# Loading the first seven blocks of grouped rows in attention's last slot instead of at the start of the expert phase

## What is computed

```
x = layernorm(x + attention(x))
x = layernorm(x + cross_attention(x, ctx))
scores = (x @ router_w.T + router_b) / temp          # 8 numbers for each token
gates  = sinkhorn(scores, 3 iterations)              # over groups of tokens and experts
top 2 gates of each token, divided by their sum
y[token] = sum over its 2 experts e: gate * ((relu(x @ wg[e]) * (x @ wp[e])) @ wo[e])
x = layernorm(x + (x + y))
```

## Time and profile before

| what | value |
|---|---|
| median of 3 runs | 991.87 us (991.46 to 995.86) |
| the profiled execution, its own time | 997.48 us |
| its span, first to last instruction | 995.7 us |
| outside the span (997.48 - 995.7) | 1.78 us |
| attention, up to the barrier | 0 to about 788 us |
| expert phase | about 788 us to the end |
| TensorE busy | 875.5 us, 88% of the span |
| mean granted TensorE clock | 0.947 of full speed |

### The profile page before, as it was taken

How to read it: one execution, slowest core, us unless ns; L and a number is a source line. 1 busy time by engine, 2 the same in 40 slices (tenths; PEclk the granted TensorE clock), 3 DMA queues, 4 the chain that set the end, 5 groups by cost and what they waited for, 6 DMA issues and landing times. The chain is left out here.

```text
span 995.7 us, 23083 instructions
## 1 busy us (share of the span) xinstructions
PE 875.5 (88%) x6694; PEld 680.1 (68%) x6694; DVE 733.4 (74%) x2148; ACT 686.6 (69%) x2423; POOL 566.7 (57%) x862
## 2 busy tenths in 40 slices
PE   4999999999999999999999987899997499989830
PEld 3777777777777777777777766677775366767620
DVE  3578888888888888888887888888886267645655
ACT  3687888878888888888887885687884154535410
POOL 5665555555555555555555554788884034777371
PEclk8999999999999999999999999899997599989975
DMA  4990000000000000000000000010000321142223
GB/s 126 253 102 11 10 8 8 8 10 8 8 13 8 8 8 8 8 11 8 9 13 6 10 9 7 20 34 31 24 21 20 84 72 36 51 136 97 67 91 116
DMA packets 63299, 39.17 MB, mean 39 GB/s; under 512 B 15904, under 2 KB 60192, under 8 KB 63232
## 3 DMA queue, kind: packets, MB, share of 16 engines
q1 hardware_dynamic: 58688, 28.89, 13.1%
q0 software_dynamic: 4544, 9.45, 2.8%
HBM read 21.51 MB, written 16.81 MB: 38 GB/s over the span
## 5 line engine op out<-in xcount | busy, mean ns | idle before, releaser
L458 ACT ACTIVATE prob<-ps,negmax 128x128 f32<-128x128 f32 x512 | 181.3, 413 | 9.5 <-DVE negmax L577 9.5
L378 POOL TENSOR_TENSOR prob<-prob,recip 128x512 f32<-128x512 f32 x128 | 136.9, 1078 | 42.4 <-DVE recip L582 42.3
L466 ACT ACTIVATE xprob<-ps,xmax 128x128 f32<-128x128 f32 x512 | 144.8, 421 | 20.0 <-DVE xmax L577 20.0
L387 POOL TENSOR_TENSOR qk_sin<-qk,sin_sb 128x128 f32<-128x128 f32 x256 | 115.5, 471 | 59.4 <-ACT qk L445 59.0
L458 ACT ACTIVATION_READ_ACCUMULATOR prob<-ps,negmax 128x1 f32 x512 | 130.0, 254 | 0.0
L577 DVE TENSOR_REDUCE xmax<-ps 128x4 f32<-128x512 f32 x128 | 87.3, 689 | 33.2 <-PE ps L866 32.9
L1475 POOL DMA_INDIRECT answered<-ysb,goes_to x78 | 76.3, 978 | 57.6 <-DVE ysb L1557 40.8
L445 ACT ACTIVATE qk<-ps 128x512 f32<-128x512 f32 x128 | 74.1, 605 | 49.3 <-PE ps L783 49.2
L393 POOL TENSOR_TENSOR qk<-qk_cos,qk_sin 128x256 f32<-128x256 f32 x128 | 94.5, 739 | 20.2 <-DVE qk_cos L586 20.2
L402 POOL TENSOR_TENSOR ve<-mv,eps 128x1 f32<-128x1 f32 x64 | 12.1, 189 | 159.2 <-DVE mv L600 158.8
L781 PE MATMUL ps<-w_lo,xT_hi 128*128 128x512 f32 x192 | 91.4, 476 | 7.4 <-DVE xT_lo L611 7.4
(11 more groups left out here) (204 smaller groups left out, 2253.4 us busy)
## 6 DMA issues: line engine op xcount, KB each, us to landing
xg<-placed SPq DMA_DIRECT2D x8, 528.0 KB, 7.5
yq<-answered SPq DMA_DIRECT2D x8, 512.0 KB, 3.9
placed<-blank_x SPq DMA_DIRECT2D x1, 3008.0 KB, 26.5
xf<-in_x SPq DMA_DIRECT2D x32, 64.0 KB, 1.9
xres<-in_x SPq DMA_DIRECT2D x32, 64.0 KB
cx<-in_ctx SPq DMA_DIRECT2D x32, 64.0 KB, 1.8
out_y<-yo SPq DMA_DIRECT2D x8, 256.0 KB, 2.4
placed<-blank_x SPq DMA_DIRECT2D x1, 1984.0 KB, 23.2
```

The costliest lines, as they stand in the source:

```text
L378: nc.gpsimd.tensor_tensor(prob[:, n], prob[:, n], recip[:, n, :, None].broadcast_to([128, 4, S]), ALU.mult).then_inc(normed, 1)
L387: last = nc.gpsimd.tensor_tensor(sines[:, :, side, :], part[:, :, 1 - side, :], table, ALU.mult)
L458: last = nc.scalar.activation(prob[:, n, j, :], bank(name)[:, j * S:(j + 1) * S], ACT.Exp, bias=negmax[:, n, j:j + 1], accum_out=sums[:, n ...
L466: last = nc.scalar.activation(xprob[:, n, g, :], bank(name)[:, g * S:(g + 1) * S], ACT.Exp, bias=xmax[:, n, g:g + 1])
```

## The change

Seven blocks of group 0 (`AHEAD = 7`) get a buffer of their own, `xg_first`, of 128 x 7 x 132 numbers. It is allocated with the buffers that live through the whole program, and so is the semaphore `first_loaded`. SP waits for `scattered[0]` and issues the load into it in slot `B + 2`, before the barrier; this wait leaves the expert phase. The chunks of group 0 are now blocks 0 to 6, 7 to 14, 15 to 22, 23 to 30, 31 to 38 and 39 to 46, where they were 0 to 7, 8 to 15 and so on; there are still six, of which five are issued in the expert phase. `xg0` is smaller by seven blocks. A helper `rows` picks the buffer for a block. All buffers allocated behind `xg_first` start 3.7 KB further on in each partition, up to those behind `xg0`.

```
+AHEAD = 7
...
+        xg_first = keep("xg_first", [128, AHEAD, ROW])
+        first_loaded = sem("first_loaded")
...
+                if isinstance(s, int) and s == B + 2:
+                    sp.wait_ge(scattered[0], 16 * 2 * plan.size[0])
+                    sp.dma_start(xg_first[:], placed[0][0:AHEAD * 128, :].rearrange("(n p) d -> p n d", p=128)).then_inc(first_loaded, 16)
...
-        xg = [sb(f"xg{g}", [128, plan.blocks[g], ROW]) for g in range(G)]
+        xg = [sb(f"xg{g}", [128, plan.blocks[g] - (AHEAD if g == 0 else 0), ROW]) for g in range(G)]
+
+        def rows(g, c0, c1):
+
+            if g == 0:
+                return xg_first[:, c0:c1, :] if c1 <= AHEAD else xg[0][:, c0 - AHEAD:c1 - AHEAD, :]
+            return xg[g][:, c0:c1, :]
+
...
-        chunks = [(g, c, min(c + CHUNK, plan.blocks[g])) for g in range(G) for c in range(0, plan.blocks[g], CHUNK)]
+        chunks = [(0, 0, AHEAD)]
+        chunks += [(g, c, min(c + CHUNK, plan.blocks[g])) for g in range(G) for c in range(0 if g else AHEAD, plan.blocks[g], CHUNK)]
...
-        xg_loaded = [sem(f"xg_loaded{n}") for n in range(len(chunks))]
+        xg_loaded = [first_loaded] + [sem(f"xg_loaded{n}") for n in range(1, len(chunks))]
...
             for n, (g, c0, c1) in enumerate(chunks):
-                if c0 == 0:
+                if n == 0:
+                    continue
+                if g and c0 == 0:
                     sp.wait_ge(scattered[g], 16 * 2 * plan.size[g])
-                sp.dma_start(xg[g][:, c0:c1, :], placed[g][c0 * 128:c1 * 128, :].rearrange("(n p) d -> p n d", p=128))\
+                sp.dma_start(rows(g, c0, c1), placed[g][c0 * 128:c1 * 128, :].rearrange("(n p) d -> p n d", p=128))\
                     .then_inc(xg_loaded[n], 16)
...
             def x_transpose(i):
                 g = plan.group_of[i]
+                j = i - plan.block0[g]
                 pe.wait_ge(xg_loaded[chunk_of[i]], 16)
                 wait(pe, lo_done, i)
-                nc.tensor.transpose(ps[:, XT, 0:128], xg[g][:, i - plan.block0[g], 0:D], ident[:]).then_inc(xt_filled, 1)
+                nc.tensor.transpose(ps[:, XT, 0:128], rows(g, j, j + 1)[:, 0, 0:D], ident[:]).then_inc(xt_filled, 1)
```

More of the change, by code:

```diff
@@ L107, in decoder_layer @@
                         [(temp_sb[:], temp), (eidx_sb[:], eidx)], tri, ones, fw_hi, fw_lo, fwo_sb,
-                        f_loaded, fo_loaded, f_hi, f_lo, fwg, fwp, fwo, plan, routing, placed, cleared, scattered)
-        ffn_phase(nc, sem, ps, routing, plan, x2_all, fw_hi, fw_lo, fwo_sb, ident, mhalf, eps, f_lo, fo_loaded, placed, answered,
+                        f_loaded, fo_loaded, xg_first, first_loaded, f_hi, f_lo, fwg, fwp, fwo, plan, routing, placed, cleared, scattered)
+        ffn_phase(nc, sem, ps, routing, plan, x2_all, fw_hi, fw_lo, fwo_sb, ident, mhalf, eps, f_lo, fo_loaded, xg_first, first_loaded, placed, answered,
                   cleared, scattered, out)
@@ L114, in attention_phase @@
                     xcos, xsin, ident_d, causal_d, gsel_d, wqkv, wo, xwq, xwkv, xwo, rw, rb, also_loaded, tri, ones,
-                    fw_hi, fw_lo, fwo_sb, f_loaded, fo_loaded, f_hi, f_lo, fwg, fwp, fwo, plan, routing, placed, cleared, scattered):
+                    fw_hi, fw_lo, fwo_sb, f_loaded, fo_loaded, xg_first, first_loaded, f_hi, f_lo, fwg, fwp, fwo, plan, routing, placed, cleared, scattered):
     with ExitStack() as phase:
@@ L1358, with ffn_phase @@
 DISPATCH_SLOT = _s + 1
-def ffn_phase(nc, sem, ps, routing, plan, x2_all, fw_hi, fw_lo, fwo_sb, ident, mhalf, eps, f_lo, fo_loaded, placed, answered,
+def ffn_phase(nc, sem, ps, routing, plan, x2_all, fw_hi, fw_lo, fwo_sb, ident, mhalf, eps, f_lo, fo_loaded, xg_first, first_loaded, placed, answered,
               cleared, scattered, out):
```

8 lines of the change are left out of this document (4 added, 4 removed).

## The result

The changed kernel takes 991.80 us in the median of 14 runs (986.98 to 992.27). The kernel before, run beside it, takes 994.53 us (14 runs, the three known beforehand among them, 991.24 to 997.72). The ratio is 0.9965, with a 95% interval of 0.9948 to 0.9981. That is 3.5 us less, the distance of the means (the medians are 2.7 us apart), and within the 0.5% that the prediction calls no change. The predicted gain, 0.40%, is inside the interval. The predicted time, 987.9 us with a range of 985.6 to 990.6, is not: 991.80 lies 1.2 us above its upper end.

What follows compares the result with a forecast made beforehand. The prediction took PE's wait for xg's load between attention and block 0, with everything behind it hanging on block 0, to bound the kernel. Terms 4.0 + 0 + 0 + 0 + 0 = 4.0 us gave 987.9 us, range 985.6 to 990.6.

Steps and rivals of the forecast that it cites:

- What bounds the kernel: Between attention and block 0, PE waits 6.49 us: barrier and register load keep 2.5, the load of xg alone 4.0.
- The load leaves the hole: Issued on SP before the barrier at about 773.1 us, it lands by 778 to 782.5; PE's wait shrinks by 4.0 us.
- The terms taken at nothing: Other loads, SP's wait for the scatters, meta one block earlier, the clock, and buffers 3.7 KB further on: 0 each.
- The five other loads: Issued behind the barrier from 788.43 us; blocks 7 to 14 land with 5 to 9 us of slack, cost 0.
- The clock: At the expert phase's start, PE's lower clock level lasts 4.5 us as before, cost 0; bounds 1.7 gained, 1.5 lost.
- the clock stays low longer: Rival, start of expert phase: clock rises at 798.0 us as before, gain shrinks to 2.5 us, 989.4 us; 14%.
- Code behind the barrier: Rival: ACT or DVE must fetch instructions for block 0 behind the barrier, gain 1.6 to 3.2 us, 989.5 us; 8%.
- The gain doesn't reach the end: Rival: group 1's scatters or the sends behind them go by something else than block 0, gain 0, 991.9 us; 7%.
- the last sentence of the sum: Whole kernel: the same 4.0 us subtracted from the median of the runs, 991.87 - 4.0 = 987.9 us, 0.40% less.

Runs made afterwards that it cites:

- the after trace with the late clock: The changed kernel, unchanged, timed and profiled again against the kernel before: 990.14 us (12 runs), ratio 0.9946; in its trace the clock rose 9.3 us after b0.
- The filler: The kernel before plus 18 matmuls that nothing reads, in slots 33 and 34 where PE waits: 989.85 us (11 runs), ratio 0.9941.

## Why the prediction was right, and where it was wrong

**What bounds the kernel: right.** The hole, the barrier in it and the register load behind it were read as they are. After: the barrier opened 1.39 us after attention's last matmul, as before, and the transpose came 786.68 - 785.55 = 1.13 us later, where the prediction said 1.1.

**The load leaves the hole: right.** 3.97 us against 4.0. The last scatter of group 0 started at 769.57 and the load was issued at 771.88, 2.31 us later, where the prediction had 2.29. It landed in 3.6 us where the rows had offered 5.0 to 9.4: those loads had others beside them, this one had none. The slack made the difference harmless.

**The terms taken at nothing: right.** Undoing the load's place alone gave 1.0005, which bounds buffers, addresses and `meta` together. The five other loads land in 5.3 to 8.5 us, and PE had no wait at block 7:

```profile
L1461 SPq DMA_DIRECT2D xg<-placed x5: 373/1007/2947, 785.6 to 790.7; - x5
...
DMA to landing us min/median/max: 5.3/7.2/8.5
```

The experiment with one block ahead shows what stood behind this zero: with too few blocks the next load is late and the gain is gone.

**The clock: the stretch too short, its price too high.** The stretch at the lower level behind b0 was taken at the 4.5 us of before. It was 4.1, 9.3 and 4.2 us in the three traces of the changed kernel. So "the clock stays low longer", given 14%, came true in one of them, at 9.3 us for the 8.5 that it named, and in nine of the 13 traces with a shorter hole. Its price was taken from one matmul, 784 against 493 ns, 0.37 us for each; between two traces of one kernel it was 0.24. The likely reason is that the waits for ACT and DVE between the matmuls don't shrink with the clock (ACT's `x_hi` takes 0.28 us and DVE's `x_lo` 0.29 at either level). The longest stretch thus costs (10.5 - 4.5) x 0.24 = 1.4 us, near the bound of 1.5 that was given. In the means nothing of it is to be seen, as the clocks above show. The Trainium skill ("TensorE: Matmul & The Clock Gate", What's actually happening) says that the length of the slow start varies from run to run, by about half a microsecond. That it varies, 4.1 and 9.3 us in two traces of one kernel agree; the size they contradict, and the measurement decides.

**Code behind the barrier: refuted.** ACT began 0.03 us behind the transpose, DVE's `x_lo` 0.03 us behind ACT, no later than in the kernel before. The Trainium skill ("Runtime: NRT & Kernel Launch", Instruction fetch mechanics) has a taken branch out of the held pages stop an engine; no trace here shows an engine held so behind this barrier.

**The gain doesn't reach the end: refuted.** The first scatter of group 1 started 56.35 us after b0, before 56.51 (57.55 in the after trace with the late clock), and the sets of runs show the 4.2 us at the end.

**The step that failed is the last sentence of the sum.** The profiled execution was called 5.6 us over the median "by something that the hole doesn't explain", and the 4.0 us were then subtracted from the median of three, 991.87. It was that median which was off, and not a cost, a wait or an overlap: in the comparison itself the kernel before has 994.53, 2.7 us more. The other 1.3 us of the miss (991.80 - 987.9 = 3.9) are that the two medians lie 2.7 us apart and not 4.0. Of 120 runs of the kernel before, 18 lie at or under 991.87, 15%; a median of three is that low in 3 x 0.15^2 x 0.85 + 0.15^3 = 6% of draws. The mean of the 120 is 994.7, and 994.7 - 4.0 = 990.7 is what the changed kernel takes (990.5). The numbers at hand would have done: the three runs and the profiled execution, 991.46, 991.87, 995.86 and 997.48, have a mean of 994.2, which gives 990.2, inside the stated range; the measured 991.80 would still be 1.6 us above it.

**With it failed the range.** It took in the terms of the sum and not the scatter of the executions themselves, "a microsecond or so". A single execution of this kernel scatters by 2.1 us, so that even a median of 14 wanders: the changed kernel's three sets have medians of 991.80, 990.14 and 989.97. The first is the highest because nine of its 14 runs stand between 991.2 and 992.3, and the other five between 986.98 and 990.21. By an estimate from the 2.1 us, a mean of four is known to 1.05 us and a median of 14 to 0.7, together 1.3; twice that, two and a half microseconds up and down, was needed for the level alone.

**Where the scatter comes from is in part known.** Over 106 runs of the kernel before with a recorded clock, the time falls by 0.5 us for each 0.001 of mean granted clock, with a correlation of -0.89; the 38 runs of the changed kernel give the same 0.5 and -0.92. Over this span 0.001 of mean clock is 2 us at the lower level, so each of them costs 0.25 us, as the 0.24 between two traces. In the 17 traces of the study, the last two slots took 25.0 to 31.0 us, the start up to the first scores 81.9 to 85.8, slots 23 to 27 135.0 to 137.1, the expert phase 197.4 to 202.5; slots 28 to 32 were 108.9 to 109.1 in all. In the first trace of before PE was busy for 65, 81, 87 and 72% of the four that vary and 96% of the one that doesn't: the scatter is in stretches where PE has pauses. The filler, which closed some of those of the last slots, took 3.3 us off them in the mean. That it did not narrow the spread shows that they are not its only source. What decides in one execution which way it goes was not found.

## What to carry to other kernels

A load whose source is complete before a barrier belongs ahead of the barrier, in a buffer that outlives it, and it needs only as many rows as are worked until the next load has landed; what it gains is the hole less the steps that stay in it (here barrier and register load, 2.5 of 6.5 us). A predicted time needs its base as much as its gain: take all executions that are known, the profiled one too, and put their own scatter into the range; subtracting a well-founded 4 us from a median of three that lies 3 us low gives a wrong time from right reasons. Where a profile shows the clock low in a stretch of sparse work, as in front of this barrier, that stretch can be worth as much as the wait behind it.

## What the runs showed of the hardware

- **POOL's drain holds the barrier.** After the small layer-norm step it took 3.96 us in every trace that has it, ended 0.95 us behind DVE's, and the barrier opened 0.18 us later. After the indirect DMAs alone it took 5.4 us, but had been over for 9 us when DVE's ended.
- **Landing times.** With no other load behind them, 66 KB landed in 1.8 us, 198 KB in 2.6 and 462 KB in 3.5 to 3.6. As the first of several, 528 KB took 4.2 to 6.1 us and 132 KB 3.5 in the first hole, 2.2 and 2.3 in the second. So alone the time goes by the size; among others the size explains only a part of it.
- **Idle matmuls can pay.** With 18 matmuls that nothing reads in the sparse last slots, these ran for the most part at the higher level, and the whole became 5 us shorter in the mean.
- **The clock can rise late behind a shorter wait.** With a hole of 5 us or less instead of 6 or more, nine of 13 traces had the rise 7.6 to 10.5 us after block 0, not 4.5 to 5.3. At 0.24 us for each microsecond such a late rise costs about one, by an estimate.
- **Traces of one program.** Three traces of the changed kernel have spans of 988.4, 993.6 and 986.1 us, 7.5 us apart, two of the kernel before 3.1, with no instruction different. A difference of that size between two single traces is not yet a finding.
